# Random-feature angles kept in turns: two steps moved from VectorE to GpSimd, range reduction cut to two VectorE operations, cosine through the absolute value on ScalarE

## What is computed

```python
shell = x @ W_shell.T + b_shell
shell = shell / max(norm(shell), 1e-12)
proj  = shell @ omega.T + rff_bias            # 32 angles for each token, in radians
phi_s = concatenate([cos(proj), sin(proj)]) * rff_scale
phi_c = mags * q ** arange(5)                 # q = tanh(charge), five powers
phi   = (phi_c outer phi_s) @ W_combine.T     # 64 features for each token
logits = (phi @ phi.T) * T / temp             # causal, 512 x 512, then softmax and V
```

## Time and profile before

| what | value |
|---|---|
| median of 3 runs | 726.18 us |
| span of the profiled execution | 729.0 us |
| TensorE busy | 707.8 us, 97% |
| VectorE busy | 620.3 us, 85% |
| ScalarE busy | 424.9 us, 58% |
| GpSimd busy | 387.0 us, 53% |
| chain that ended last, share of TensorE | 85% |

### The profile page before, as it was taken

One profiled execution on the slowest core, in us unless ns is written; L12 is line 12 of the kernel. 1 busy time (PEld: TensorE's weight loads), 2 busy tenths in 40 slices (PEclk: granted clock), 3 DMA queues, 4 the chain that ended last, 5 costly groups with the idle time before them and its releaser, 6 DMA issues.

```text
span 729.0 us, 15002 instructions
## 1 busy us (share of the span) xinstructions
PE 707.8 (97%) x4592; PEld 558.7 (77%) x4592; DVE 620.3 (85%) x1899; ACT 424.9 (58%) x840; POOL 387.0 (53%) x828
## 2 busy tenths in 40 slices
PE   7998999999999999999999999999999999999896
PEld 4977777777797887778697787879788777867684
DVE  5887888788989898998989899898989899887865
ACT  4539475736456584656648574655757565565441
POOL 4526577363565646476564747556574646653300
PEclk9889999999999999999999999999999999999999
DMA  7341111112423050323214042322304132121004
GB/s 217 112 145 43 45 28 32 29 31 65 111 89 87 6 155 16 116 59 117 58 47 129 3 125 51 116 58 79 98 1 144 31 117 59 59 59 59 1 7 167
DMA packets 49110, 54.12 MB, mean 74 GB/s; under 512 B 6214, under 2 KB 40584, under 8 KB 49032
## 3 DMA queue, kind: packets, MB, share of 16 engines
q1 hardware_dynamic: 48258, 52.64, 25.7%
q10 hardware_dynamic: 774, 0.53, 0.3%
HBM read 20.65 MB, written 16.78 MB: 51 GB/s over the span
## 4 chain that ended last, share of the span: by engine, by line
PE 85%; DVE 5%; DMA 2%; ACT 2%; POOL 2%; issue 2%; SPq 0%; DVEq 0%; ACTq 0%; POOLq 0%
PE ps L438 17%; PE ps L317 16%; PE ps L343 15%; PE ps L466 6%; PE ps L409 6%; PE ps L515 5%; PE ps L500 4%; PE ps L579 4%; PE ps L388 4%; PE ps L559 2%; PE ps L478 2%; POOL Z L254 2%; PE ps L390 2%; DMA xmT<-Z 1%; DMA X<-in_x 1%
## 5 line engine op out<-in xcount | busy, mean ns | idle before, releaser
L438 PE MATMUL ps<-VS,ET 128*128 128x257 f32 x640 | 159.4, 383 | 0.8 <-ACT ET L769 0.5
L438 PEld LDWEIGHTS ps<-VS,ET 128*128 128x128 f32 x640 | 112.5, 189 | 24.3 <-issue 11.7
L254 POOL TENSOR_TENSOR Z<-Z,QB 128x512 f32<-128x512 f32 x60 | 76.5, 1275 | 98.0 <-ACT Z L750 96.3
L708 ACT ACTIVATE xn<-X,rs 128x256 f32<-128x256 f32 x128 | 66.3, 592 | 73.3 <-POOL rs L1322 73.2
L769 ACT ACTIVATE ET<-ps 128x128 f32<-128x128 f32 (+3 forms) x128 | 55.2, 436 | 69.3 <-PE ps L317 67.9
L343 PE MATMUL ps<-W1h,xh 128*128 128x354 f32 x256 | 88.9, 347 | 0.2 <-DVE xl L889 0.2
L902 DVE TENSOR_TENSOR VS<-ps,biasM 128x354 f32<-128x354 f32 x128 | 66.3, 522 | 24.8 <-PE ps L343 24.7
L759 ACT ACTIVATE E<-ps,nmax 128x128 f32<-128x128 f32 (+3 forms) x128 | 64.3, 525 | 35.7 <-DVE nmax L971 34.2
L343 PE MATMUL ps<-W1l,xh 128*128 128x354 f32 x256 | 84.2, 329 | 0.0
L343 PE MATMUL ps<-W1h,xl 128*128 128x354 f32 x256 | 83.3, 325 | 0.0
L264 POOL TENSOR_SCALAR xm<-X,rs 128x256 f32<-128x256 f32 x120 | 65.8, 562 | 4.7 <-POOL rs L1343 4.7
(11 more groups left out here) (210 smaller groups left out, 1678.9 us busy)
## 6 DMA issues: line engine op xcount, KB each, us to landing
X<-in_x SPq DMA_DIRECT2D x32, 512.0 KB, 4.3
xmT<-Z SPq DMA_DIRECT2D x120, 128.0 KB, 2.3
out_x<-X SPq DMA_DIRECT2D x30, 512.0 KB, 3.9
out_x<-X SPq DMA_DIRECT2D x4, 256.0 KB, 2.2
X<-in_gru_whhT SPq DMA_DIRECT2D x1, 768.0 KB
wih<-in_gru_wihT SPq DMA_DIRECT2D x1, 768.0 KB
X<-in_W_v ACTq DMA_DIRECT2D x1, 256.0 KB, 4.3
X<-in_W_outT ACTq DMA_DIRECT2D x1, 256.0 KB, 5.0
```

Of the source, the lines that this page charges most:

```text
L254: e.tensor_tensor(Z[:, i + 1, :], Z[:, i, :], QB[:, :], ALU.mult).then_inc(s["zm"], 1)
L438: ins = e.matmul(p[:, 0:D + 1], ET[:, r % 2, j * 128:j * 128 + 128], VS[:, (2 * k + d) % 4, j, 0:D + 1], start=j == 0, stop=j == i)
L708: ins = e.activation(xn[:, d, t, :], X[:, b % NX, t, :], ACT.Identity, bias=rs[:, d, 2, t:t + 1], scale=rs[:, d, 1, t:t + 1])
```

## The change

The angles are counted in turns instead of radians. At setup the columns 322 to 353 of the weights, their bias and `biasS` are scaled by 1/(2 pi). `phase(k)` goes from VectorE to GpSimd, right behind `rnorm(k)` and ahead of `slot_change(m)` and `power(p,0)`. On VectorE the call of `turns(k)` stays where it was and now holds two operations, one that adds and subtracts MAGIC and one subtraction; `unwind` and `clamp` are gone. ScalarE's `sine` has three activations instead of two: an Abs, the Sin for the sine, and the Sin for the cosine of the absolute value. The orders of the calls are otherwise the same, written with numbers in place of `NP`.

```diff
 sine(k), ScalarE:
                 e.wait_ge(s["trig"], k + 1)
                 e.wait_ge(s["q_t"], k + 1)
                 to = PS[:, :, :, :].rearrange("p t b r -> p b t r")
-                e.activation(to[:, :, :, 0:R], tg[:, :, :, 0:R], ACT.Sin, bias=quarter[:, 0:1])
-                e.activation(to[:, :, :, R:2 * R], tg[:, :, :, R:2 * R], ACT.Sin).then_inc(s["sin"], 1)
+                e.activation(tg[:, :, :, 0:R], tg[:, :, :, R:2 * R], ACT.Abs).then_inc(s["fold"], 1)
+                e.activation(to[:, :, :, R:2 * R], tg[:, :, :, R:2 * R], ACT.Sin, scale=SCALE)
+                e.wait_ge(s["fold"], k + 1)
+                e.activation(to[:, :, :, 0:R], tg[:, :, :, 0:R], ACT.Sin, bias=quarter[:, 0:1],
+                             scale=-SCALE).then_inc(s["sin"], 1)
 turns(k), VectorE:
                 e.wait_ge(s["p2"], k + 1)
-                e.tensor_scalar(angles(trn), angles(ang), 1.0 / TWO_PI, MAGIC, ALU.mult, ALU.add).then_inc(s["p3"], 1)
-                e.wait_ge(s["p3"], 5 * k + 1)
-                e.tensor_scalar(angles(trn), angles(trn), -MAGIC, None, ALU.add).then_inc(s["p3"], 1)
+                e.tensor_scalar(angles(trn), angles(ang), MAGIC, -MAGIC, ALU.add, ALU.add).then_inc(s["p3"], 1)
+                e.wait_ge(s["p3"], k + 1)
+                e.tensor_tensor(rows(tg)[:, :, R:2 * R], rows(ang), rows(trn), ALU.subtract).then_inc(s["trig"], 1)
 GpSimd:
+            def phase(k):
+                e.wait_ge(s["rn"], k + 1)
+                if k == 0:
+                    e.wait_ge(s["soft"], SOFT)
+                i = (2 * k) % 4
+                e.tensor_tensor(ang[:, :, :, :], VS[:, i:i + 2, :, 322:354],
+                                n2[:, :, 0, :].unsqueeze(3).broadcast_to([128, 2, 4, R]),
+                                ALU.mult).then_inc(s["p1"], 1)
+                e.wait_ge(s["p1"], k + 1)
+                turn = ang[:, :, :, :].rearrange("p d t r -> p (d t) r")
+                e.tensor_tensor(turn, turn, biasS[:, :].unsqueeze(1).broadcast_to([128, 8, R]),
+                                ALU.add).then_inc(s["p2"], 1)
...
-                lm_norm(f, 1); square(p, 1); rnorm(p); slot_change(m); power(p, 0); power(p, 1)
+                lm_norm(f, 1); square(p, 1); rnorm(p); phase(p); slot_change(m); power(p, 0); power(p, 1)
 setup, VectorE:
-                    e.tensor_copy(W1[:, c, 322:354], at["setup_mm", c][:, 322:354]).then_inc(s["setup_evac"], 1)
+                    e.tensor_scalar(W1[:, c, 322:354], at["setup_mm", c][:, 322:354], 1.0 / TWO_PI, None,
+                                    ALU.mult).then_inc(s["setup_evac"], 1)
...
-                e.tensor_copy(biasM[:, 257:354], at["setup_mm", 2][:, 257:354]).then_inc(s["setup_evac"], 1)
+                e.tensor_copy(biasM[:, 257:322], at["setup_mm", 2][:, 257:322]).then_inc(s["setup_evac"], 1)
+                e.tensor_scalar(biasM[:, 322:354], at["setup_mm", 2][:, 322:354], 1.0 / TWO_PI, None,
+                                ALU.mult).then_inc(s["setup_evac"], 1)
```

More of the change, by code:

```diff
@@ L80 @@
 rz_mm grz srz gx_mm rhn gn nn hd hz sn aT_t aT   sv_mm sv   of_mm fin
-q1 q_t qb z_t zc zm zs
-p1 p2 sin2 dm8 mk
+q1 q_t qb z_t zc zm zs fold
+p1 p2 dm8 mk
 ln_r ln_b
@@ L636, in _ @@
[L636 to L640, removed]
@@ L656, in _ @@
[L656 to L659, removed]
-                p, n, f, m, g = it + 2, it + 1, it, it - 1, it - 2
[L661 to L668, removed]
@@ L1277, in _ @@
-            top(2, 0, 1); shift(2, 0); gates(1); top(2, 1, 0); candidate(1); top(2, 1, 1); attended(3, 4)
-            shift(2, 1); new_slots(1); lm_stats(3, 2); attended(3, 5); chosen(2, 0); weight_sum(2, 0)
-            for it in range(3, NP - 1):
+            xn_low(0, 0, 1); bias_setup(); xn_low(0, 1, 0); ln_stats(1, 1, 0); vs(0, 0, 0); ln_stats(1, 1, 1)
+            vs(0, 0, 1); vs(0, 0, 2); xn_low(0, 1, 1); vs(0, 0, 3); square_a_setup(); norm_sum(0, 0)
+            xn_low(1, 0, 0); vs(0, 1, 0); xn_low(1, 0, 1); vs(0, 1, 1); attention_setup(); vs(0, 1, 2)
@@ new lines, in _ @@
+            ln_stats(3, 0, 1); row_max(0, 4); turns(1); row_max(0, 5); attended(0, 0); xn_low(2, 0, 0)
+            row_max(0, 6); attended(0, 1); attended(0, 2); attended(0, 3); row_max(0, 7); lm_stats(0, 0)
+            attended(0, 4); ln_stats(3, 1, 0); attended(0, 5); xn_low(2, 0, 1); attended(0, 6)
+            ln_stats(3, 1, 1); lm_stats(0, 1); lm_stats(0, 2); lm_stats(0, 3); lm_stats(0, 4); lm_stats(0, 5)
+            vs(2, 0, 0); ln_stats(4, 0, 0); vs(2, 0, 1); lm_stats(0, 6); xn_low(2, 1, 0); qk_full(1)
@@ new lines, in _ @@
+            xm_low(1, 0, 0); row_max(2, 0); row_max(2, 1); row_max(2, 2); vs(3, 1, 0); vs(3, 1, 1)
+            row_max(2, 3); vs(3, 1, 2); vs(3, 1, 3); chosen(0, 1); attended(2, 0); xm_low(1, 0, 1)
+            lm_stats(2, 0); norm_sum(3, 0); weight_sum(0, 1); xm_low(1, 1, 0); row_max(2, 4); row_max(2, 5)
+            attended(2, 1); norm_sum(3, 1); xm_low(1, 1, 1); turns(3); gathered(0); attended(2, 2)
+            attended(2, 3); row_max(2, 6); lm_stats(2, 1); xn_low(4, 0, 1); gates(0); row_max(2, 7)
@@ new lines, in _ @@
+            attended(2, 4); lm_stats(2, 2); lm_stats(2, 3); xn_low(4, 1, 0); candidate(0); attended(2, 5)
+            lm_stats(2, 4); top(1, 0, 0); lm_stats(2, 5); attended(2, 6); vs(4, 0, 0); top(1, 0, 1)
+            shift(1, 0); lm_stats(2, 6); xn_low(4, 1, 1); vs(4, 0, 1); new_slots(0); qk_full(3); top(1, 1, 0)
+            attended(2, 7); top(1, 1, 1); weight_sum(1, 0); slot_values(0); lm_stats(2, 7); row_max(3, 0)
+            shift(1, 1); chosen(1, 0); row_max(3, 1); vs(4, 0, 2); row_max(3, 2); vs(4, 0, 3); vs(4, 1, 0)
@@ L1280, in _ @@
+            gates(1); top(2, 1, 0); candidate(1); top(2, 1, 1); attended(3, 4); shift(2, 1); new_slots(1)
+            lm_stats(3, 2); attended(3, 5); chosen(2, 0); weight_sum(2, 0)
+            for it in range(3, 15):
                 p, n, f, m, g = it + 2, it + 1, it, it - 1, it - 2
@@ L1288, in _ @@
-                norm_sum(p, 0); row_max(n, 4); vs(p, 1, 1); vs(p, 1, 2); vs(p, 1, 3); lm_stats(n, 0)
-                norm_sum(p, 1); xm_low(f, 1, 0); xm_low(f, 1, 1); row_max(n, 5); attended(n, 1); phase(p)
-                turns(p); unwind(p); clamp(p); attended(n, 2); lm_stats(n, 1); new_slots(m); lm_stats(n, 2)
-                row_max(n, 6); row_max(n, 7); attended(n, 3); top(f, 0, 0); top(f, 0, 1); shift(f, 0)
-                top(f, 1, 0); top(f, 1, 1); shift(f, 1); attended(n, 4); attended(n, 5); weight_sum(f, 0)
@@ new lines, in _ @@
+                finish(g, 0, 1); row_max(n, 3); gates(m); vs(p, 0, 0); vs(p, 0, 1); vs(p, 0, 2); vs(p, 0, 3)
+                xn_low(p, 1, 0); candidate(m); attended(n, 0); xn_low(p, 1, 1); xm_low(f, 0, 0)
+                xm_low(f, 0, 1); finish(g, 1, 0); finish(g, 1, 1); vs(p, 1, 0); norm_sum(p, 0); row_max(n, 4)
+                vs(p, 1, 1); vs(p, 1, 2); vs(p, 1, 3); lm_stats(n, 0); norm_sum(p, 1); xm_low(f, 1, 0)
+                xm_low(f, 1, 1); row_max(n, 5); attended(n, 1); turns(p); attended(n, 2); lm_stats(n, 1)
@@ L1464, in _ @@
             power(3, 3); slot_change(0); shift8(1, 0); lm_scale(2, 0); shift8(1, 1); lm_norm(2, 0)
-            lm_scale(2, 1); square(4, 0); lm_norm(2, 1); square(4, 1); rnorm(4); alpha(1, 0); alpha(1, 1)
-            power(4, 0); power(4, 1); power(4, 2); shift8(2, 0); shift8(2, 1); slot_change(1); alpha(2, 0)
-            power(4, 3); alpha(2, 1)
-            for it in range(3, NP - 1):
+            lm_scale(2, 1); square(4, 0); lm_norm(2, 1); square(4, 1); rnorm(4); phase(4); alpha(1, 0)
+            alpha(1, 1); power(4, 0); power(4, 1); power(4, 2); shift8(2, 0); shift8(2, 1); slot_change(1)
```

300 lines of the change are left out of this document (127 added, 173 removed).

## The result

The changed kernel takes 731.1 us, the median of 4 runs (729.48 to 731.64), beside 726.3 us for the kernel before in the same session (4 runs, 725.48 to 726.57): a ratio of 1.0063 [1.0044, 1.0082]. It is slower by 4.8 us.

The account below looks back on a forecast made before the run. TensorE was taken to bound the loop, with ScalarE level at z_t and rt_t. Loop 3.3 + pair 1 0.64 + pairs 2 and 3 0.60 + setup 0.1 = 4.6 us on 726.18 gave 730.8 us, range 725.9 to 733.8.

Parts of the forecast that it names:

- the loop: In 11 turns the Abs delays z_t and rt_t on TensorE by 0.30 us each turn: 3.3 us, bound 4.4.
- The start: Before the loop: 0.64 us at pair 1, 0.60 at pairs 2 and 3, 0.1 for setup.
- pair 1: In the start, row_max(0,5) behind turns(1) comes 0.34 us later and the Abs adds 0.30: 0.64, bounds 0.30 and 1.0.
- GpSimd: Two products gained, 1.45 us a pair, 23 us over 16; VectorE waits some 1.2 at turns, no cost in the loop.
- VectorE: Sheds 2.6 us a pair, 42 us over 16, beside TensorE's work; attended(n,2) and what follows come 1.4 us sooner.
- VectorE's load, which the change lowers most, ends nothing inside the loop: TensorE is busy throughout the 41.8 us turn, VectorE 37.5, so lightening VectorE was held to be worth nothing there.
- an earlier trig moves nothing: At the sine, the table load starts at 348.38 before VectorE's last step ends at 348.45, so trig doesn't gate it.
- Faster: Rival: VectorE's shorter list reaches TensorE, removing start DMA waits and 0.1 us at rt_t: -3.1, 723.1 us; 10%.
- Paid back: Rival of no difference: ScalarE's 0.26 us wait for row_max(n,5) absorbs most of the Abs: 727.2 us; 17%.
- A table load of its own for the Abs: Rival on ScalarE: the Abs needs another 1.28 us load, so a turn pays 1.58: 748.8 us; 6%.
- GpSimd late: Rival: two GpSimd products take over 2.8 us, so trig comes behind the Abs's possible start: 737.4 us; 5%.
- The offset: Timed runs lie 2.8 us below the profiled span of 729.0, so 4.6 us was added to their median, 726.18.

Follow-up runs that it names:

- a_no_abs: The changed kernel without the Abs and its wait, the cosine Sin reading the unfolded angle (wrong values in half of the features): 725.03 us, ratio 0.9996.
- a_abs2: The changed kernel with a second, unused Abs of the same size ahead of the first: 733.98 us, ratio 1.0110.
- a_fold_dve: The changed kernel with the fold back on VectorE in place of the Abs: 726.91 us, ratio 1.0008.
- b_again: The kernel before, unchanged, profiled a second time: span 723.1 us, turns of 41.74 us.
- b_dve_more: The kernel before with one unused VectorE operation of 128x256 values (0.42 us) behind the fold: 730.89 us, ratio 1.0060.
- b_pool: The kernel before with only phase moved to GpSimd behind rnorm, unwind and clamp kept: 733.92 us, ratio 1.0120.
- b_dve_two: The kernel before with two unused VectorE operations of 128x256 values behind the fold: 738.97 us, ratio 1.0177.
- b_abs_mid: The kernel before with the Abs added between the two Sins, behind the table load: 732.37 us, ratio 1.0084.
- a_again: The changed kernel, unchanged, profiled a second time: span 729.6 us, turns of 42.07 us.
- b_abs: The kernel before with the Abs alone added, ahead of the table load, VectorE keeping all its operations: 735.55 us, ratio 1.0129.

## Why the prediction was right, and where it was only lucky

**The forecast** of 730.8 us met 731.1, and by the mechanism that it named. TensorE at 97% was level with ScalarE at z_t; the Abs overlaps one neighbour and costs 0.30 ahead of the load (0.82 against 0.52); 0.32 to 0.34 a turn came of it. Forecast 3.3 us in the loop, measured 3.7. a_no_abs shows that there is no other term in the loop, a_abs2 that the price repeats. That the sum came within 0.3 us is partly luck: the loop was 0.4 too low, and the term of the start cannot be told from its scatter.

**The start** was forecast at 1.34 and shows 1.4, which proves little: the start of `phi(4)` lay between 186.4 (a_no_abs) and 189.1 us (a_fold_dve) for two kernels that take the time of before, neither with a half clock in the start, so its scatter is twice the term. For pair 1 the parts can be read, counted from the end of rnorm in b_again and in after: the table load 3.40 and 4.07 (forecast +0.64, measured +0.67), z_copy +0.68, `phi(1)` +0.99. Ahead of it in after:

```profile
54.42 0.61 POOL L1329 TENSOR_TENSOR ang<-VS,n 128x256 f32<-128x256 f32 x1
...
55.87 0.30 DVE L911 TENSOR_SCALAR trn<-ang 128x256 f32<-128x256 f32 x1 [1.42 <-POOL ang L1334]
...
56.55 0.55 DVE L930 TENSOR_REDUCE nmax<-ps 128x1 f32<-128x384 f32 x1
57.13 0.58 ACT L750 ACTIVATE E<-ps,nmax 128x384 f32<-128x384 f32 x1 [1.08 <-DVE nmax L930]
```

row_max(0,5) stands behind turns(1), as forecast, and expo waits for it. But a_no_abs has the GpSimd part of this delay as well (its load comes at 3.77) and is no slower than before. The DMA waits of TensorE at `phi`, forecast to grow from 1.9 to about 3 us, are 1.1 in after beside 0.4 in b_again. The setup term of 0.1 us was not measured by itself.

**GpSimd** takes 0.62 + 0.72 and the hand-offs, 1.41 us a pair against 1.45; VectorE idles 1.38 in front of turns against 1.2. The total is 406.3 us for a forecast of 409.

**VectorE** sheds 33 us and not 42. The largest missing term, 5.9 us over the 16 pairs, is L911 at 0.80 in the loop, where GpSimd's next operation runs beside it; in pair 1, where only short ones do, it takes 0.30. The other 3 us are overlap: from b_again to after the durations of VectorE's rows, added up, fall by 35.7 us and its busy time by 32.7, since neighbouring operations overlap by up to 0.1 us and busy time counts that once. The trace of before had the slower L911 in plain sight: L923 at 761 ns beside L927 at 424 for the same count of values, which I took for the price of L923's form. Its spread says otherwise (shortest, median and longest in ns):

```profile
L923 DVE TENSOR_TENSOR ang<-VS,n x16: 413/924/928, 38.2 to 637.2; 128x256 f32<-128x256 f32 x16
```

It takes 0.41 to 0.43 in pairs 0 to 4, and 0.82 to 0.93 in the 11 turns, where it runs beside slot_change. So attended(n,2) comes 1.0 us sooner (3.04 from attended(n,1), 4.06 in b_again) and not 1.4. The cover took it up. The Trainium skill (SBUF — State Buffer, section "Who interferes with whom") says that VectorE and GpSimd share a pair of ports under an exclusive lock and that the second to issue waits until the first is done; the trace agrees: L911 ends 0.14 us behind the end of L288, and is short wherever nothing long runs beside it. No run was made to test the ports as the cause.

**The step that failed** is the sentence "VectorE's load, which the change lowers most, ends nothing inside the loop". It is true only downward. a_no_abs and a_fold_dve show that a lighter VectorE gains nothing; b_dve_more, b_pool and b_dve_two show that a heavier one pays in full, 0.34, 0.57 and 0.80 us a turn. In after the weight load of e_t(n,7) starts 0.52 behind shift(f,1), in place of 0.10, and VectorE idles 0.81 us ahead of the routing step, for rt_t. I had priced the GpSimd move as free because everything behind turns came sooner, which held only together with the cut of unwind and clamp. Alone it costs 1.2%. In the same way "an earlier trig moves nothing" was right for the kernel before and wrong as a reason for this one: with the Abs ahead of the table load, trig is needed some 1.3 us sooner, at the Abs and no longer at the Sin behind the load, and VectorE's relief pays for that. The Abs alone costs 1.3% and the GpSimd move alone 1.2%; together, and with unwind and clamp gone, they cost 0.6%.

**The rivals.** "Faster" needed a pause of ScalarE ahead of the Sins; there is none. "Paid back" needed ScalarE's wait for row_max to absorb the 0.3; it did not. A table load of its own for the Abs did not come: the loads ahead of the sine are 16, one for each pair, as before. "GpSimd late" did not happen, with 0.69 us to spare.

**The offset** between span and median, 2.8 us, was taken as given. The timed runs show 1.8 us more than the span of the same execution, so the profiled execution was one of about 730.8 us, 4.6 slower than the median, most of it the half clock in the start. Since the change was added to the median, the sum did not suffer. The DMA waits of TensorE, on which I built the price of pairs 1 to 3, are no fixed term: they sum to 1.9 us in that execution and 0.4 in b_again, but also to 1.7 in b_abs_mid with the full clock in the start, and to 1.2 in a_again with 3.4 us of half clock there. What sets them stays open.

## What to carry to other kernels

When the bounding engine is busy without a gap, look at each hand-off into it, and at the weight load, not the matmul, for how much time is left between the release and the use. Engines that look 60% or 85% busy can both be level with it, each at one place. Then cutting work from them gains nothing and adding work costs its full length, and what an operation moved to the idler engine costs is decided at that place and not by the average load. An operation put ahead of a table load inherits a wait that the load used to cover. And an engine's mean duration of an operation can hide two values: look at the spread, and at what the neighbour engine does meanwhile.

## What was unexpected of the hardware

- A late release costs its whole delay, though the matmul seems to wait less: 0.09 us at four transposes was followed by 0.25 of slower steps (b_dve_more), 0.30 by 0.27 (b_pool) and 0.54 by 0.26 (b_dve_two). In all three the weight load had lost its lead of 0.22 us on the matmul.
- The table load is not held by the wait of the Sin behind it (it ran under L953), but an Abs in the program's order ahead of the Sin is not moved behind the load; in b_abs it held the load up by 0.62 us.
- The Trainium skill (ScalarE: Activation LUTs, section "What ACT_TABLE_LOAD costs") counts 1.38 us of draining with a switch of tables; here the load starts 0.02 us behind the end of the Abs (344.68 + 0.43 to 345.13) and the Sin 0.02 behind the load.
- A 128x256 operation with one input on VectorE took 0.80 us beside a GpSimd operation of 0.73, and 0.28 to 0.30 where none or only short ones ran beside it (after).
- A stretch of 3.4 us at half clock in the tail cost about 1.6 us (78.3 us in after, 76.6 in a_again and 76.7 in b_again).
